# Twelve-stage network on one core: expert stages turn x itself, and results are scattered to rows of their own

## The reference, cut to what matters

```python
sorted_indices = jnp.argsort(-expert_mask, axis=0)[:cap]
used_idx = (sorted_indices * sorted_mask).reshape(-1)
h = jax.nn.relu(jnp.einsum('ceh,ehi->cei', inputs, experts_inter))
out = jnp.einsum('cei,eih->ceh', h, experts_out) * in_w[..., None]
combined = jnp.zeros_like(x_flat).at[used_idx].add(out.reshape(-1, hidden))
combined = combined + x_flat * (noop_w * noop_mask)[:, None]
```

## Time and profile before

| | |
|---|---|
| median of three runs | 2909.27 us |
| the profiled execution, its own time | 2918.43 us |
| its span | 2916.7 us |
| busy PE, DVE, ACT, POOL | 2341.5, 2014.7, 1870.3, 969.9 us |
| granted clock of TensorE, mean | 0.878 |
| ffn0 stages start at | 44.8 and 318.6 us |
| the stages after them start at | 210.4 and 483.7 us |
| ffn3 stages start at | 2037.3 and 2816.3 us |
| the stage after the first of them starts at | 2136.2 us |

### The profile page before, as it was taken

The page is one execution under the profiler, slowest core; times in us unless marked ns, Lnnn a source line. Parts: engine busy times, 40 slices in busy tenths (PEclk is TensorE's granted clock), DMA queues, the critical chain, the costliest instruction groups (busy, mean ns, idle before and its releaser), DMA issues. The chain is left out here.

```text
span 2916.7 us, 44003 instructions
## 1 busy us (share of the span) xinstructions
PE 2341.5 (80%) x13097; PEld 1224.7 (42%) x13097; DVE 2014.7 (69%) x5787; ACT 1870.3 (64%) x4763; POOL 969.9 (33%) x1288
## 2 busy tenths in 40 slices
PE   4647574828888878499999999997858888888878
PEld 4425453612222236344444444444524444444453
DVE  3605641769999956666666666665579999999855
ACT  2114323327777773467777777776549999999975
POOL 2562276254344332500000000003544444444437
PEclk8777686559999995699999999999779999999989
DMA  6330232022323200000000000000011111111000
GB/s 168 84 56 1 89 65 46 1 41 53 75 49 67 63 12 1 30 1 1 1 1 1 1 1 1 1 1 1 1 34 30 30 30 30 30 30 28 4 1 29
DMA packets 230508, 86.76 MB, mean 30 GB/s; under 512 B 175426, under 2 KB 223362, under 8 KB 230274
## 3 DMA queue, kind: packets, MB, share of 16 engines
q1 hardware_dynamic: 215168, 74.74, 11.1%
q0 software_dynamic: 9856, 7.58, 2.0%
q10 hardware_dynamic: 5250, 1.62, 0.3%
HBM read 26.47 MB, written 15.50 MB: 14 GB/s over the span
## 5 line engine op out<-in xcount | busy, mean ns | idle before, releaser
L2406 ACT ACTIVATE s_pT<-s_ps_t 128x512 f32<-128x512 f32 x1024 | 626.3, 639 | 140.4 <-PE s_ps_t L1995 124.0
L2154 DVE TENSOR_REDUCE s_neg_max<-s_ps_a 128x1 f32<-128x512 f32 x1024 | 666.8, 683 | 63.0 <-PE s_ps_a L1961 53.1
L2397 ACT ACTIVATE s_first<-s_ps_a,s_neg_max 128x512 f32<-128x512 f32 x512 | 391.5, 765 | 24.5 <-DVE s_neg_max L2154 23.0
L2007 PE MATMUL s_ps_t<-ident,s_first 128*128 128x128 f32 x2048 | 316.5, 285 | 82.0 <-ACT s_pT L2406 69.4
L2737 DVE CUSTOM_DVE_ANT_0 s_e<-s_ps_a,w_alibi 128x128 f32<-128x128 f32 (+3 forms) x512 | 231.1, 489 | 189.8 <-PE s_ps_a L2583 189.6
L2325 POOL TENSOR_SCALAR s_first<-s_first,s_rec 128x512 f32<-128x512 f32 x128 | 232.3, 1815 | 366.4 <-DVE s_rec L2160 360.4
L2853 ACT ACTIVATE s_e<-s_e,s_neg_max 128x128 f32<-128x128 f32 (+3 forms) x512 | 283.0, 555 | 43.0 <-DVE s_neg_max L2737 41.4
L1961 PE MATMUL s_ps_a<-s_lanesT 64*128 64x512 bf16 x1024 | 275.8, 401 | 37.4 <-DMA s_lanesT<-n_lanes 20.5
L2007 PEld LDWEIGHTS s_ps_t<-ident,s_first 128*128 128x128 f32 x2048 | 221.3, 142 | 181.4 <-ACT s_pT L2406 139.3
L2025 PE MATMUL s_ps_o<-s_pT,n_v_pad 128*32 128x512 f32 x2048 | 277.6, 616 | 12.2 <-ACT s_oT L2412 12.2
L2863 ACT ACTIVATE s_pT<-s_ps_t 128x512 f32<-128x512 f32 (+3 forms) x512 | 195.6, 434 | 124.1 <-PE s_ps_t L2595 123.8
(11 more groups left out here) (382 smaller groups left out, 4136.8 us busy)
## 6 DMA issues: line engine op xcount, KB each, us to landing
s_token_rows<-s_rows SPq DMA_DIRECT2D x4, 1088.0 KB, 5.4
s_x_rows<-x SPq DMA_DIRECT2D x4, 1024.0 KB, 5.3
x<-s_x_rows SPq DMA_DIRECT2D x8, 512.0 KB, 6.0
s_Wi<-L_ffn_experts_inter SPq DMA_DIRECT2D x2, 1792.0 KB, 8.1
x<-L_attn_x SPq DMA_DIRECT2D x4, 512.0 KB, 8.0
out<-x SPq DMA_DIRECT2D x8, 256.0 KB, 2.3
s_lanesT<-n_lanes SPq DMA_TRANSPOSE x64, 4.6
s_shiftedT<-n_lanes SPq DMA_TRANSPOSE x64, 2.4
```

The source lines that it names most:

```text
L2007: last = pe.transpose(st[n % NK][:, t * P:(t + 1) * P], first[:, p % NF, 2 * t + a, i * P:(i + 1) * P], G.ident[:])
L2154: dve.tensor_reduce(neg_max[:, column(n):column(n) + 1], sa[n % NA][:], AX.X, ALU.max, negate=True).then_inc(s.max_ready, 1)
L2397: act.activation(first[:, g % NF, n % PU, :], sa[n % NA][:], ACT.Exp, bias=neg_max[:, n:n + 1], accum_out=sum1[:, n % (NR * PU):n % (NR * ...
L2406: act.activation(pT[:, n % NP, :], st[n % NK][:], ACT.Exp).then_inc(s.probs_ready, 1)
```

## The change

In setup TensorE multiplies the router, the gates and M by `I - 1/128` (`center`), so a product with them takes the mean out of x by itself. In both kinds of stage TensorE then turns x, not xn, and the deviation (`rstd`) is multiplied into the logits, in ffn3 also into the mask. ffn3 has two PSUM buffers for turning (one is the fifth of y), no xn, and `choose` in four pieces, half 1's put between the additions.

In ffn0 xn is still made, for the gathered rows and the own share, after the turning. A token's two choices are told apart (`second`, `told_tile`, `to_index`), and each result goes to a row of its own in `y_rows`, a table of 2 x 4608 rows, by a scatter that only writes. The table's used part is zeroed first, by two DMAs of SP. x stays in SBUF: DVE adds the own share tile by tile between the experts, and at the end `add_rows` adds both tables in eight pieces, loaded through four buffers. `number` shifts and masks integers. There are four gather buffers, three experts gathered before the first scatter. Wi and Wo are loaded after the rows are stored.

```diff
+pe.wait_ge(s.made, 3)
+pe.wait_ge(router.router_loaded, 32)
+pe.matmul(psC[:, 0:KINDS], center[:], raw_router[:], start=True, stop=True).then_inc(s.router_psum, 1)
 multiply_linear(pe)
+pe.wait_ge(linear.gate_loaded, 16)
+pe.wait_ge(s.router_copied, 1)
+pe.matmul(psC[:, 0:KINDS], center[:], raw_gate[:], start=True, stop=True).then_inc(s.gate_psum, 1)
 turn_adapters(pe)
+center_linear(pe, center)
...
+dve.wait_ge(s.router_psum, 1)
+dve.tensor_copy(G.routerT[:], psC[:, 0:KINDS]).then_inc(s.router_copied, 1)
 combine_adapters(dve)
 make_signatures(dve)
+halve_linear(dve)
+dve.wait_ge(s.gate_psum, 1)
+dve.tensor_copy(G.gateT[:], psC[:, 0:KINDS]).then_inc(s.gate_copied, 1)
+copy_adapters(dve)
 copy_linear(dve)
-copy_adapters(dve)
...
+    for i in range(2):
+        pe.wait_ge(s.m_halved, i + 1)
+        pe.matmul(ps[i][:], center[:], M[:, 4 * i:4 * i + 4, :], start=True, stop=True).then_inc(s.centered_psum, 1)
+def copy(dve):
+    for i in range(2):
+        dve.wait_ge(s.centered_psum, i + 1)
+        dve.tensor_copy(G.M[:, 4 * i:4 * i + 4, :], ps[i][:]).then_inc(s.m_copied, 1)
...
+turned = [turned_ps[:], y[NY - 1][:].rearrange("p e d -> p (e d)")]
...
-def choose(h):
+def shift_logits(h):
     at, wide = half(h), [P, WT, E]
     dve.wait_ge(s.logits_psum, HB * (h + 1))
-    do(dve.tensor_copy(logits[:, at], logits_ps[h][:, 0:WT * E].rearrange("p (t e) -> p t e", e=E)))
+    dve.wait_ge(s.rstd_ready, HB * (h + 1))
+    do(dve.tensor_tensor(logits[:, at], logits_ps[h][:, 0:WT * E].rearrange("p (t e) -> p t e", e=E),
+                         N.rstd[:, at].unsqueeze(2).to_broadcast(wide), ALU.mult))
...
-top2_mask(do, dve, T, probs[:, at], mask[:, at], WT)
...
+do(dve.tensor_tensor(mask[:, at], mask[:, at], N.rstd[:, at].unsqueeze(2).to_broadcast(wide), ALU.mult))
...
-for h in range(HALVES):
-    choose(h)
+shift_logits(0)
+divide(0)
+first_expert(0)
+second_expert(0)
 for t in range(0, NT, 2):
     for e in range(E // 2):
         add_expert(t, e)
         add_expert(t + 1, e)
+    if t == 0:
+        shift_logits(1)
+    if t == 4:
+        divide(1)
+    if t == 6:
+        first_expert(1)
+    if t == 8:
+        second_expert(1)
...
-pool.wait_ge(s.rstd_ready, b + 1)
-do(pool.tensor_tensor(minus[:, at], N.mv[:, at, 0], N.rstd[:, at], ALU.mult))
-do(pool.tensor_scalar(minus[:, at], minus[:, at], -1.0, None, ALU.mult))
-pool.engine_nop().then_inc(s.minus_ready, 1)
...
-normalise(0)
 for b in range(B):
-    if b + 1 < B:
-        normalise(b + 1)
-    copy_xnT(b)
-for h in range(HALVES):
-    exp(h)
+    copy_xT(b)
+exp(0)
 for t in range(NT):
+    if t == 3:
+        exp(1)
     weigh_others(t)
...
-for t in range(TB):
-    last = pe.transpose(turned_ps[:, t * P:(t + 1) * P], xn[:, b % 2, t, :], G.ident[:])
...
+if b >= 2:
+    pe.wait_ge(s.xT_ready, b - 1)
+for t in range(TB):
+    last = pe.transpose(turned[b % 2][:, t * P:(t + 1) * P], G.x[:, b * TB + t, :], G.ident[:])
...
-NX = 3
+NX = 4
...
-sp.dma_start(Wi[:], inp["L0_ffn_experts_inter"].rearrange("e d i -> d e i")).then_inc(s.experts_loaded, 16)
-sp.dma_start(Wo[:], inp["L0_ffn_experts_out"].rearrange("e (c p) d -> p e c d", p=P)
-             ).then_inc(s.experts_loaded, 16)
-sp.dma_start(by_tile(x_rows)[:, NT:, :], G.x[:, NT:, :]).then_inc(s.x_stored, 16)
+sp.wait_ge(s.zeros_set, 1)
+for c in range(2):
+    sp.dma_start(y_rows[c * ROWS:c * ROWS + B * L].rearrange("(p n t) d -> p n (t d)", p=P, t=TB),
+                 zeros[:].unsqueeze(1).to_broadcast([P, B, TB * D])).then_inc(s.y_cleared, 16)
 sp.wait_ge(s.empty_set, 1)
 sp.dma_start(by_tile(token_rows)[:, NT:, :], empty[:]).then_inc(s.empty_stored, 16)
 for h in range(HALVES):
     sp.wait_ge(s.rows_ready, h + 1)
     sp.wait_ge(s.xn_ready, WT * (h + 1))
     sp.dma_start(by_tile(token_rows)[:, half(h), :], rows[:, half(h), :]).then_inc(s.rows_stored, 16)
-for h in range(HALVES):
-    sp.wait_ge(s.x_ready, WT * (h + 1))
-    sp.dma_start(by_tile(x_rows)[:, half(h), :], G.x[:, half(h), :]).then_inc(s.x_stored, 16)
-sp.wait_ge(s.x_stored, 16 * (HALVES + 1))
+sp.dma_start(Wi[:], inp["L0_ffn_experts_inter"].rearrange("e d i -> d e i")).then_inc(s.experts_loaded, 16)
+sp.dma_start(Wo[:], inp["L0_ffn_experts_out"].rearrange("e (c p) d -> p e c d", p=P)
+             ).then_inc(s.experts_loaded, 16)
 for q in range(Q):
     sp.wait_ge(scattered[q], 16 * E)
+for n in range(2 * B // 2):
+    c, i = n % 2, n // 2
+    if n >= 4:
+        sp.wait_ge(s.x_added, n - 3)
+    sp.dma_start(parts[:, n % 4].rearrange("p (t d) -> p t d", d=D),
+                 by_tile(y_rows[c * ROWS:(c + 1) * ROWS])[:, 2 * TB * i:2 * TB * (i + 1), :]).then_inc(loaded[n % 4], 16)
 for i in range(4):
-    tiles = slice(i * NT // 4, (i + 1) * NT // 4)
-    sp.dma_start(G.x[:, tiles, :], by_tile(x_rows)[:, tiles, :]).then_inc(s.x_loaded, 16)
-sp.wait_ge(s.x_loaded, 64)
+    sp.wait_ge(loaded[i], 16 * B // 4)
...
+last = pe.transpose(turned_ps[b % 2][:, t * P:(t + 1) * P], G.x[:, b * TB + t, :], G.ident[:])
...
+find_slots(2)
 turn(0)
+find_slots(3)
 upward(0)
-find_slots(2)
 for e in range(E):
-    if e + 3 < E:
-        find_slots(e + 3)
+    if e + 4 < E:
+        find_slots(e + 4)
     downward(e)
     if e + 1 < E:
...
-                     G.router_b[:].unsqueeze(1).to_broadcast(wide), ALU.add))
+                     N.rstd[:, at].unsqueeze(2).to_broadcast(wide), ALU.mult))
+do(dve.tensor_tensor(logits[:, at], logits[:, at], G.router_b[:].unsqueeze(1).to_broadcast(wide), ALU.add))
...
-def keep_own(h):
-    do(dve.tensor_copy(noop[:, half(h)], rows[:, half(h), D + E]))
-    for t in range(h * WT, (h + 1) * WT):
-        dve.scalar_tensor_tensor(out=G.x[:, t, :], in0=xn[:, t, :], scalar=noop[:, t:t + 1],
-                                 in1=G.x[:, t, :], op0=ALU.mult, op1=ALU.add).then_inc(s.x_ready, 1)
+def keep_own(t):
+    dve.scalar_tensor_tensor(out=G.x[:, t, :], in0=xn[:, t, :], scalar=noop[:, t:t + 1],
+                             in1=G.x[:, t, :], op0=ALU.mult, op1=ALU.add).then_inc(s.x_kept, 1)
+def add_rows(n):
+    i = n // 2
+    if n == 0:
+        dve.wait_ge(s.x_kept, NT)
+    if n % 2:
+        dve.wait_ge(s.x_added, n)
+    x = G.x[:, 2 * TB * i:2 * TB * (i + 1)].rearrange("p t d -> p (t d)")
+    dve.wait_ge(loaded[n % 4], 16 * (n // 4 + 1))
+    dve.tensor_tensor(x, x, parts[:, n % 4], ALU.add).then_inc(s.x_added, 1)
...
-do(dve.tensor_tensor(incl[:], te(prefix), incl[:], ALU.add))
-do.free(dve.scalar_tensor_tensor(out=kept[:], in0=incl[:], scalar=float(CAP), in1=mask[:],
+do(dve.scalar_tensor_tensor(out=number_i[:], in0=te(prefix), scalar=-1.0, in1=incl[:],
+                            op0=ALU.add, op1=ALU.add))
+do.free(dve.scalar_tensor_tensor(out=kept[:], in0=number_i[:], scalar=float(CAP - 1), in1=mask[:],
                                  op0=ALU.is_le, op1=ALU.mult))
-def steps(to, width, n):
-    do(dve.tensor_scalar(to, incl[:], float(width), None, ALU.is_gt))
-    for i in range(2, n):
-        do(dve.scalar_tensor_tensor(out=to, in0=incl[:], scalar=float(width * i), in1=to,
-                                    op0=ALU.is_gt, op1=ALU.add))
-    do(dve.scalar_tensor_tensor(out=incl[:], in0=to, scalar=float(-width), in1=incl[:],
-                                op0=ALU.mult, op1=ALU.add))
-steps(in_tile[:], P, Q)
-steps(quarter[:], QUARTER, P // QUARTER)
-do.free(dve.scalar_tensor_tensor(out=quarter[:], in0=in_tile[:], scalar=float(P // QUARTER),
-                                 in1=quarter[:], op0=ALU.mult, op1=ALU.add))
-do(dve.tensor_tensor(code[:].rearrange("p e t -> p t e"), incl[:], kept[:], ALU.mult))
+do.free(dve.tensor_scalar(quarter[:], number_i[:], 5, None, ALU.arith_shift_right))
+do(dve.tensor_scalar(place[:], number_i[:], QUARTER - 1, None, ALU.bitwise_and))
+do(dve.scalar_tensor_tensor(out=code[:], in0=place[:], scalar=1.0, in1=kept[:],
+                            op0=ALU.add, op1=ALU.mult))
+do(dve.scalar_tensor_tensor(out=told_tile[:], in0=second[:], scalar=float(SECOND),
+                            in1=tile_no[:].unsqueeze(2).to_broadcast([P, NT, KINDS]),
+                            op0=ALU.mult, op1=ALU.add))
...
+do(dve.tensor_scalar(is_second[:], slots[:, 0], float(SECOND), None, ALU.is_gt))
+do(dve.scalar_tensor_tensor(out=row[:], in0=row[:], scalar=float(-P), in1=none[:],
                             op0=ALU.add, op1=ALU.add))
+do(dve.scalar_tensor_tensor(out=index[:, e, :], in0=is_second[:], scalar=float(-P * SECOND), in1=row[:],
+                            op0=ALU.mult, op1=ALU.add))
 dve.engine_nop().then_inc(s.index_ready, 1)
+dve.scalar_tensor_tensor(out=to_index[:, e, :], in0=is_second[:], scalar=float(ROWS - P * SECOND), in1=row[:],
+                         op0=ALU.mult, op1=ALU.add).then_inc(s.to_index_ready, 1)
...
+mark(3)
+read_slots(2)
+read_slots(3)
 dve.wait_ge(s.xn_ready, NT)
-keep_own(0)
-keep_own(1)
+do(dve.tensor_copy(noop[:], rows[:, :, D + E]))
 for e in range(E):
-    if e + 3 < E:
-        mark(e + 3)
-    if e + 2 < E:
-        read_slots(e + 2)
+    if e + 4 < E:
```

(41 more changed lines are left out.)

115 lines of the change are left out of this document (66 added, 49 removed).

## The result

The changed kernel took **2903.73 us** (median of 20 runs, 2893.73 to 2913.67) beside 2911.01 (2907.9 to 2916.21) for the kernel before: ratio 0.9975, 95% interval 0.9966 to 0.9984. It is 7 us faster, where 51 were forecast, and lies 26 us above the end of the range. Its profiled execution is the slowest of the twenty: 2913.67 us, span 2911.9. The record doesn't name the chip of these runs; from here on it is "the record's chip", and "the record" in a comparison means this profile.

A forecast was written before the change was run, and what follows sets the result against it. Bounds: in linear stages a late head and gap, then TensorE; in capacity stages one chain, then GpSimd at 12.4 us an expert. 25.6 + 27.8 - 2.3 = 51.1 off the median 2909.3 gives 2858 us, range 2842 to 2878.

The forecast's parts named there:

- TensorE goes at its own 9.49 us if GpSimd keeps up: Capacity stages: with three experts gathered ahead, TensorE sets a 9.49 us period per expert; SP starts 23.7 us earlier.
- its charge of 1.5 us: Capacity stages, each: 1.5 us lost because long GpSimd issues beside DVE's marking can hold up the first scatters.
- capacity stages, both: First and third of twelve stages, routed experts with capacity: 27.8 us gained together.
- linear stages, both: Tenth and twelfth stages, linear experts: earlier start, no gap after five products; 12.8 us gained each, 25.6 together.
- setup: Setup: two centring products and their copies after the adapters' turn, partly overlapped, 2.3 us lost.
- 13.9: Net gain of each capacity stage in us: 23.7 less 1.5 for long issues and 8.3 for the longer end.
- A: Rival, capacity stages: plain scatter still costs GpSimd 1.55 us, 12.4 an expert; 12 us lost in all, 2870; chance 0.26.
- B: Rival, capacity stages: the weights' transfer collides with first gathers, and reading pauses at the end; 2870 us; chance 0.12.
- D: Rival, capacity stages: weights, last in SP's queue, arrive late; at 75 GB/s 30 us late in each, 2918; chance 0.02.
- C: Rival, both kinds of stage: turning goes at 2.4 GHz, granted clock above 0.5; 12 us faster, 2846; chance 0.10.
- E: Rival, all four stages: something waits as long as before, so time stays within 6 us of 2909; chance 0.02.
- The other rule: Capacity stages: by the skill's lockout rule only each marking's 0.35 us step costs, at most 2.5 us over seven.

The follow-up runs named there:

- e9: The changed kernel, unchanged, timed again on chip C: 2868.00 us, ratio 0.9842 to the kernel before.
- e10: The changed kernel with scatters that add into the zeroed tables, on chip C: 2882.46 us, ratio 0.9894.
- e17: The changed kernel with scatters that add into the zeroed tables, on chip B: 2885.69 us, ratio 0.9906.
- e16: The changed kernel, unchanged, timed again on chip B: 2872.17 us, ratio 0.9852 to the kernel before.
- e3: The changed kernel with Wi and Wo loaded ahead of the zeroing instead of behind the rows, on chip A: 2903.58 us, ratio 0.9988.
- e14: The kernel before with scatters that only write, the addition left out, on chip D: 2909.68 us, ratio 0.9984.
- e5: The kernel before with scatters that only write, the addition left out, on chip B: 2875.62 us, ratio 0.9880.
- e12: The changed kernel, unchanged, timed again on chip D: 2900.29 us, ratio 0.9956 to the kernel before.
- e18: The changed kernel with each gather issued only when the one before has landed, on chip B: 2910.79 us, ratio 0.9985.

## Why the prediction was wrong, point by point

**The step that failed** is "TensorE goes at its own 9.49 us if GpSimd keeps up", with its charge of 1.5 us. GpSimd did keep up, and TensorE did not go at its own pace on the record's chip: in the first stage the first weighing came 74.9 us in (forecast 67.4), and the six periods behind it made 72.0 us (forecast 56.9 and the 1.5), 21 us too long together of the 21.4 that the stage missed. In their place the runs showed late signals; what makes them stays open. Of the profile's miss of 46.3 us (2911.9 against 2916.7 - 51.1 = 2865.6), the capacity stages hold 43.9, the linear ones 5.2, the setup -0.8 and the rest -2.0.

| term | forecast | record | chips B, C |
|---|---|---|---|
| capacity stages, both | 27.8 gained | 16.1 lost | 26.2 gained (e9) |
| linear stages, both | 25.6 gained | 20.4 | 21.0 (e9) |
| setup | 2.3 lost | 1.5 lost | 1.3 lost (e9) |
| time | 2858 (2842 to 2878) | 2903.7 | 2868.0, 2872.2 |

**Its steps in a capacity stage**, by e9, where they can be seen. The head: forecast first weighing 67.4 us into the stage, measured 65.5; the exponential was back 19.2 into the stage of the record's profile (21.0 before), numbering took 4.26 us against 4.5 forecast, with integer shift and mask at 0.28 each, below my 0.42. The plain scatter: 0.95 taken, 0.97 to 1.0 in most rows and 1.04 in the mean. The pace: six periods made 60.7 us, forecast 56.9 and the 1.5; the first two were 10.2 and 13.1 and the rest 9.35. Before the long one, five additions of the own share and the marking beside a 1.81 us scatter made the slot products late (128.51), and the downward products behind them went at a lower clock (5.47 us at 129.41 instead of 3.84); that the one brought the other is argued, no run separates it. SP began 133.5 us into the stage (forecast 131.5 and the 1.5), and from there to the next stage it was 19.3 us, forecast 18.6. So 13.9 was nearly right for a chip without late signals: 12.8 and 13.4.

**In a linear stage** the head was 1.1 us better than forecast (first product at 19.0, forecast 20.1), and the body 2.9 worse: 64 products took 64.8 us from 2072.55 where five in 6.0 and 59 at 3.72 a pair, with 1.0 charged, make 61.9. Two gaps of 2.7 us together stand where I had charged 1.0: half 1's choice delayed additions more than five buffers hide. The pair period was 3.79. These are the tenth stage's; the twelfth gained 9.4, 3.4 less than forecast.

**The rivals.** A is out: scatters cost 1.04 at most in the mean. Its price of 12 us for the adding form was near, 14.5 (e10 less e9) and 13.5 (e17 less e16). B and D are out: in the record's profile the weights had landed by 97, before the upward product at 101.88, and the first gather was 3.1 us earlier than before. e3, which takes the weights out of that place, was no better. C is out, though 0.55 is above the 0.5 that the prediction named as its sign: TensorE was busy 18.65 of 18.90 us, the clock was at 0.89 in the first 2.4 us (2053.6 to 2056.0), and then at 0.50, the lower level of 1.2 GHz, for the other 16.5, in which TensorE was busy without a break. By the rule that I cited from the Trainium skill (TensorE: Matmul & The Clock Gate, "What's actually happening") it should have come; the rows of before spoke against it, and so do these. E, "something in each of the four stages waits as long as before" with 0.02, is nearest by its number (5.5 below 2909.3), but that is luck: the linear stages did what they should, and what waited in the capacity stages was nothing that had waited before. I had read the profile for prices and waits, but the rows had 9.49 us an expert even beside gathers (116.66 to 145.14) and no late signal; nothing was put down for TensorE's work with the gathers beside it not being handed on in time. I had one execution's trace and took it for every chip's.

**The other rule**, that GpSimd's writing of descriptors is locked out by two-port copies of DVE (the Trainium skill, SBUF — State Buffer, "Who interferes with whom"), doesn't explain the long issues here. Those of 1.82 us (99.11, record) and 1.81 (127.45, e9) begin when the marking's `tensor_scalar` has ended (98.97, 127.27), and lie beside the one-hot's 1.22 us `tensor_tensor` (98.89, 127.18). The 1.5 us charged for such issues can't be read off by itself. The same section says that TensorE and ScalarE never wait on anyone; on chips B and C the traces agree. On D and the record's chip TensorE's results reached DVE microseconds after its records' ends (2.1 to 3.6 us in the record), and its own instructions paused; the traces don't show whether a port had to do with it.

## What to carry to other kernels

Run the kernel under study itself in every lot of experiments, and on more than one chip, before a mechanism is looked for in the code: two chips gave this change 7 to 14 us and two gave it 43 to 46, and a kernel that another engine bounds (here the one before, by GpSimd's adding scatters) takes the same time on all. Scatters to rows of their own pay where the adding scatter bounds, 13 to 15 us on the chips where it was tried (B and C). What they uncover is TensorE's chain, and on D the plain form gave the kernel before only 5 us (e14), on B 37 (e5). A period read beside the same gathers on one chip, 9.49 us here, was no promise for another.

## What the runs showed of the hardware that was not expected

- The same program differs by 1.0 to 1.2% between chips (2868.0 and 2872.2, 2900.3 and 2903.7), the kernel before by 0.2% (2910.2 to 2915.6). On A, D and the record's chip signals of TensorE reach DVE late, in the record 2.1 to 3.6 us after its records' ends (133.48 against 131.39, 105.55 against 101.95), in stretches with indirect gathers; DVE idles 42 us more there than in e9.
- The clock is lower where TensorE pauses: in 112 to 140 us the granted clock was 0.85 and 0.89 with late signals (record, e12) and 0.94 without (e9, e16).
- An indirect DMA of 128 rows takes GpSimd 0.94 us to gather, 0.97 to scatter, 1.55 to scatter with addition; gathers and plain scatters that begin beside DVE's 1.22 us one-hot take 1.8 (98.62 and 127.45 in e9).
- Pacing gathers by their landing costs 38.6 us (e18 against e16): each lands 1.8 to 1.9 us after its issue has ended.
